# Attention's instruction order: from slots written out per unit to an order made by a list scheduler at build time

## The chip, the cores and the metric

The kernel runs on one core of one Trainium2 chip. The time is the device time of one execution in microseconds. The kernel before took 3646.02 us, the median of 3 runs (3645.23 to 3649.91).

## The reference

One post-norm transformer layer, in float32, on x of shape 2 x 2048 x 1024:

```python
q  = (x @ Wq) as 32 heads of 32;   k, v = x @ Wkv   # one shared key/value head of 32
scores = q k^T / sqrt(32) + slope[head] * (key - query), causal
a  = softmax(scores) @ v                            # then concatenated to 1024
x  = layernorm(x + a @ Wo)
x  = layernorm(x + x @ W^T + b + lora(x))           # lora: one of 4 ranks, chosen per token by a gate
```

## The kernel before

**Work and stages.** The kernel has two parts, one after the other: `attention` and `feed_forward`. Only `attention` changes. It is cut into 64 *units*. A unit `g` is 512 queries (a *segment*, `seg_of(g) = g // 8`) by 4 heads; there are 8 segments (4 for each of the 2 sequences) with 8 units each. Because of causality a unit of the s-th segment of its sequence (s = 0, 1, 2, 3) has `ktiles(g)` = 4, 8, 12 or 16 key tiles of 128 keys. The prediction calls these the four quarters; each quarter occurs twice, so each has 16 units. The last 4 key tiles of a unit lie on the diagonal and have 512, 384, 256 and 128 live query columns.

**What a unit does.** All matrix products are made of a high and a low part to reach float32 accuracy.

1. *Projection* `Q`: q for 4 heads, 8 chunks of the model dimension times 3 products, 24 products of 512 columns, into the bank `ps_m` (L782 to L784, `three`). ScalarE takes the high part (`QE`, L565), VectorE the low part (L671); SyncE copies it within `qst` by DMA.
2. *Maxima* `A`: q times all keys with queries on the partitions, only to find the row maximum (L816, banks `ps_a`), 16 products per segment of keys. VectorE reduces each (L682; on the diagonal with a mask, L685). `CV` and `CT` (L691, L823, L697) turn the result into a shift row, sent by a small DMA.
3. *Scores* `S`: for each key tile and head one product with keys on the partitions (L895, banks `ps_s`, at times `ps_m` as a third), plus a mask product on the diagonal (L898). ScalarE takes the exponential into one of 8 probability tiles `prob` (L603).
4. *Value products* `PV`: per key tile a group of 4 heads, each head on its own 32 columns of the array (128 x 32 weights `val`), float32 in two passes: 8 matmul rows (L828, `ps_o`).
5. *Sums of probabilities*: the same shape with ones for weights (L828, `ps_sum`). `SM` sums one key tile. `SP` sums a pair that GpSimd has added before (`ADD`, L540), `SQ` a quad made of two added pairs (`ADDQ`, L545). A probability tile is free again when its sum is done (`sm_done`, waited for by ScalarE at L602).
6. *End*: ScalarE copies `ps_o` (`OE`, L608), VectorE inverts the sums (`R`), GpSimd multiplies (L521), SyncE stores.

In the sixth unit of a segment x of the next segment is transposed as well (`X`, L777, through the `ps_a` banks), and its keys and values are projected into `ps_m` (`KV`, `VT`). Near the end the 8 pieces of Wo are split into high and low parts (`WO`, L594, L751).

**What sets the order.** Each engine takes its instructions strictly in the order of its queue. `plan_unit(g)` writes that order for one unit; all engines walk the same list and pick what is theirs. The backbone is one score product per slot. Everything else is hung at slots by tables with one entry per quarter: `Q_AT`, `QE_AT`, `A_END`, `A_FROM`, `CHUNKS_AHEAD`, `PV_AT`, `SM_AT`, `WS_AT`, `KV_AT` and others. While unit `g` makes its scores, maxima of `g + 1` (and some of `g + 2`) and the projection of `g + 2` are made. A value product stands after the score of head `PV_AT` of the next key tile, the sum after that of head `SM_AT`:

```python
PV_AT = (1, 1, 2, 1)
SM_AT = (2, 1, 2, 1)
QUADS = (0, 0, 0, 1)   # quads per unit in each quarter; further pairs: pairs_summed
```

With `pairs_summed(g)` = 0, 3, 5, 7 the number of sum groups per unit is 4, 5, 7 and 8. A projection enters the queue as 3 products at a time, the keys' and values' 24 in one piece. `score_places()` fixes which bank each score goes to.

The functions that the diff touches, with the line numbers of the profile:

## Time and profile before

| | |
|---|---|
| median of 3 runs | 3646.02 us |
| profiled execution: span of its instructions | 3641.2 us |
| attention, to the last value product | 2789 us |
| preparation of the feed-forward part | 81 us |
| its 32 tiles of tokens | 771 us |
| TensorE, VectorE, ScalarE, GpSimd busy | 96%, 63%, 51%, 39% |
| granted TensorE clock, mean | 0.988 |

The profile comes from one execution. For it there is the span from the first to the last instruction, 3641.2 us; no separate device time is given, so its own time is this span beside the median of the runs, which is 4.8 us above it. TensorE (PE) rows have modelled ends: two neighbouring products can overlap in the rows, and only the distance from start to start tells what one costs. PEld is the loading of weights, which overlaps with products. A wait is written as *who <- released by whom*. GpSimd is POOL, VectorE DVE, ScalarE ACT; L numbers are lines of the kernel.

### The profile page before, as it was taken

The numbers are of one execution on the slowest core, as the hardware profiler recorded it, in microseconds if no ns is written. First come the engines' busy times: TensorE is split into PE (matmuls) and PEld (weight loads), VectorE is DVE, ScalarE is ACT, GpSimd is POOL, SyncE is SP. The second block draws the span as 40 slices with busy tenths as digits, with TensorE's granted clock in tenths as the row PEclk, the third lists the DMA queues.
The fourth block names the chain that finished last, engine by engine and source line by source line (L and its number), as shares of the span: only waits on it lengthen the run. The fifth ranks groups of instructions, "written<-read, shape, count | busy, mean of one in ns | idle before, by whom it ended". The sixth has DMA issues, their size and how long they took to land. (4 is left out here: it accounts for less than half of the span.)

```text
span 3641.2 us, 56102 instructions
## 1 busy us (share of the span) xinstructions
PE 3481.5 (96%) x20833; PEld 2190.3 (60%) x20833; DVE 2290.6 (63%) x5375; ACT 1866.5 (51%) x3188; POOL 1431.2 (39%) x435
## 2 busy tenths in 40 slices
PE   5999999999999999999999999999998999999998
PEld 4555555555454554555555555454544899999997
DVE  4577777776777772677777776777762444455444
ACT  2546656665667666546656665667675101111100
POOL 1115444554657556115444554657574101011010
PEclk8999999999999999999999999999998999999999
DMA  2221110001000010221110000000012122121221
GB/s 79 55 61 30 35 48 24 25 24 42 18 19 19 19 41 19 57 62 30 36 48 24 24 24 19 19 19 18 13 58 83 47 69 65 56 69 56 65 69 41
DMA packets 158395, 148.33 MB, mean 41 GB/s; under 512 B 9396, under 2 KB 141492, under 8 KB 156056
## 3 DMA queue, kind: packets, MB, share of 16 engines
q1 hardware_dynamic: 158168, 145.34, 13.5%
q8 instruction: 139, 2.28, 0.3%
q14 instruction: 88, 0.72, 0.1%
HBM read 94.39 MB, written 33.62 MB: 35 GB/s over the span
## 5 line engine op out<-in xcount | busy, mean ns | idle before, releaser
L603 ACT ACTIVATE prob<-ps_s,alibi 128x512 f32<-128x512 f32 (+3 forms) x2119 | 1287.2, 633 | 741.6 <-PE ps_s L895 377.9
L540 POOL TENSOR_TENSOR prob<-prob 128x2048 f32<-128x2048 f32 (+1 forms) x240 | 1047.8, 4369 | 977.7 <-ACT prob L603 977.4
L682 DVE TENSOR_REDUCE mxp<-ps_a 128x1 f32<-128x512 f32 x1536 | 978.5, 682 | 296.0 <-PE ps_a L816 284.2
L816 PE MATMUL ps_a<-wol,qst 97*128 97x512 f32 (+3 forms) x2560 | 954.8, 395 | 37.0 <-DVE mxp L685 17.6
L895 PE MATMUL ps_s<-qst,kexp 97*128 97x512 f32 (+3 forms) x2119 | 862.7, 411 | 44.2 <-ACT prob L603 28.5
L895 PEld LDWEIGHTS ps_s<-qst,kexp 97*128 97x128 f32 x2119 | 399.0, 189 | 563.8 <-ACT prob L603 321.5
L685 DVE CUSTOM_DVE_ANT_0 ps_a<-ps_a,maska 128x128 f32<-128x128 f32 (+3 forms) x1024 | 492.4, 507 | 243.8 <-PE ps_a L816 233.3
L828 PE MATMUL ps_o<-prob,val 128*32 128x512 f32 (+3 forms) x5120 | 603.5, 543 | 9.9 <-ACT prob L603 6.6
L816 PEld LDWEIGHTS ps_a<-wol,qst 97*128 97x128 f32 x2560 | 486.5, 194 | 112.7 <-DVE mxp L685 31.9
L1089 POOL TENSOR_TENSOR work<-work,bias_b 128x1024 f32<-128x1024 f32 x32 | 76.9, 2402 | 745.4 <-DVE work L1228 710.9
L828 PE MATMUL ps_sum<-prob,ones 128*32 128x512 f32 (+2 forms) x3072 | 332.5, 505 | 3.7 <-POOL prob L540 3.3
L514 POOL TENSOR_TENSOR wol<-wq_raw,wol 128x1024 fp32r<-128x1024 f32 x64 | 152.5, 2383 | 449.8 <-ACT wol L558 449.8
L603 ACT ACTIVATE prob<-ps_m,alibi 128x512 f32<-128x512 f32 (+3 forms) x441 | 255.2, 579 | 116.6 <-PE ps_m L898 75.0
L1113 ACT ACTIVATE root<-var 128x1 f32<-128x1 f32 x64 | 13.0, 203 | 581.6 <-DVE var L1172 581.6
L1295 PE MATMUL ps_z<-wth,hth 128*128 128x364 f32 x768 | 255.6, 333 | 5.4 <-DVE htl L1250 5.4
L1297 PE MATMUL ps_z<-wtl,hth 128*128 128x364 f32 x768 | 252.8, 329 | 0.0
L1299 PE MATMUL ps_z<-wth,htl 128*128 128x364 f32 x768 | 252.8, 329 | 0.0
L782 PE MATMUL ps_m<-woh,wol 128*128 128x512 f32 x576 | 232.3, 403 | 3.2 <-DVE woh L646 2.8
L784 PE MATMUL ps_m<-woh,wol 128*128 128x512 f32 x576 | 230.0, 399 | 0.0
L783 PE MATMUL ps_m<-woh,wol 128*128 128x512 f32 x576 | 228.9, 397 | 0.0
L671 DVE SCALAR_TENSOR_TENSOR qst<-ps_m,qst 32x512 fp32r<-32x512 f32 x256 | 176.1, 688 | 80.0 <-ACT qst L565 73.4
L828 PEld LDWEIGHTS ps_o<-prob,val 128*32 128x32 f32 x5120 | 105.7, 108 | 188.1 <-ACT prob L603 119.8
(129 smaller groups left out, 3994.7 us busy)
## 6 DMA issues: line engine op xcount, KB each, us to landing
wq_raw<-in_L_attn_Wq SPq DMA_DIRECT2D x64, 512.0 KB, 3.5
work<-in_L_attn_hidden_states SPq DMA_DIRECT2D x8, 2048.0 KB, 8.3
qst<-qst SPq DMA_DIRECT2D x64, 256.0 KB
att_scratch<-at_sb SPq DMA_DIRECT2D x64, 256.0 KB, 2.8
at_raw<-att_scratch SPq DMA_DIRECT2D x32, 512.0 KB, 5.2
work<-in_L_attn_hidden_states SPq DMA_DIRECT2D x32, 512.0 KB, 4.1
out<-work SPq DMA_DIRECT2D x32, 512.0 KB, 3.1
work<-in_L_attn_Wo SPq DMA_DIRECT2D x8, 512.0 KB, 4.1
```

The lines of the kernel that those rows point to most:

```text
L540: nc.gpsimd.tensor_tensor(even[:, :, c1:], even[:, :, c1:], odd[:, :, c1:], ALU.add).then_inc(pair_done, 1)
L603: nc.scalar.activation(prob[slot_of(steps + k)][:, h, c0:], ps_s[places[GH * (steps + k) + h][0]][:, c0:], ACT.Exp, bias=alibi_of(g, h, k ...
L682: nc.vector.tensor_reduce(top, ps, AX.X, ALU.max).then_inc(a_done, 1)
L685: nc.vector.tensor_tensor_reduce(ps, ps, maska[:, QB - cols:], 1.0, MASKED, ALU.add, ALU.max, top).then_inc(a_done, 1)
L782: nc.tensor.matmul(ps, wh, mh, start=start, stop=False)
L784: return nc.tensor.matmul(ps, wl, mh, start=False, stop=stop)
L816: last = nc.tensor.matmul(ps[:, 0:cols], qst[buf][0:KR, h, t * P:(t + 1) * P], kmax[0:KR, ring(sg):ring(sg) + cols], start=True, stop=True)
L828: last = nc.tensor.matmul(ps[h * DH:(h + 1) * DH, c0:], weights, prob[slot_of(steps_before(g) + k)][:, h, c0:], start=k == 0, stop=k == kt ...
L895: last = nc.tensor.matmul(bank[:, c0:], kexp[0:KR, at:at + P], qst[g % 3][0:KR, h, c0:], start=True, stop=not diagonal)
L1295: nc.tensor.matmul(ps, hth[:, c], wth[:, c, piece(p)], start=c == 0, stop=False, skip_group_check=True)
L1297: nc.tensor.matmul(ps, hth[:, c], wtl[:, c, piece(p)], start=False, stop=False, skip_group_check=True)
L1299: last = nc.tensor.matmul(ps, htl[:, c], wth[:, c, piece(p)], start=False, stop=False, skip_group_check=True)
```

## The change

`plan_unit`, `score_places` and their tables go. A class `Order` makes one list of items for all units and all engines at build time. It keeps a clock for each engine, the time at which each bank, probability tile and loaded weight is free, and puts down one piece after the other: for TensorE whatever `choose` names next, for the other engines what follows from it (`push` at the time when its input is ready by the builder's own constants). The instructions that an item issues are those of before, with these differences:

- `QUADS` is (0, 0, 1, 2).
- The 24 products of a projection, of q as of keys and values, are 24 items.
- Value products and sums are taken in batches; a score or a maximum goes to whichever bank of its kind is free first, with the waits for that bank's last user; `ps_m` serves as third score bank when no projection needs it within 2 us.
- The five VectorE steps of the keys (`take_kv`) are five items, with a gap of 700 ns between them; so are the heads of q (300 ns), transposes of x (500 ns) and pieces of Wo (4 us).
- `stack_in` is split into `slopes_in` and `stack_in`; `invert` has two more waits; maxima of a unit may start as soon as its q is there, up to two units ahead of the scores.

```diff
-CHUNKS_AHEAD = (7, 14, 18, 19)
-... (all the tables, chunks_ahead, third_from, score_places, plan_unit)
-QUADS = (0, 0, 0, 1)
+QUADS = (0, 0, 1, 2)
+class Order:
+    S_BANKS, A_BANKS, M_BANK = (0, 1), (2, 3, 4), 5
+    FILL, DRAIN, LOAD, MODE_IN, MODE_OUT = 0.4567, 163, 104, 93, 90
+    SHORT, BATCH, MOST, PACE, MARGIN = 30, 3, 5, 30, 2000
+    LOOK, NARROW_SLACK = 100, 50
+    QE_GAP, X_GAP, K_GAP, WO_GAP = 300, 500, 700, 4000
+    def wide(self, at, length):
+        begin = max((max(self.pe + self.MODE_OUT, at) if self.narrow else max(self.began, at)) + self.LOAD, self.pe)
+        self.narrow, self.began, self.pe = False, begin, begin + length
+        return begin + max(length, 60) + self.DRAIN
+    def columns(self, at, n):
+        begin = max(self.pe + (0 if self.narrow else self.MODE_IN), at + 30)
+        self.narrow, self.began, self.pe = True, begin, begin + 2 * (n * 0.833 + 7)
+        return self.pe + 165
+    def m_open(self):
+        return not self.m_held and self.project_from() > self.pe + self.MARGIN
+    def do_s(self):
+        g, k, h = self.s_unit, self.s_tile // GH, self.s_tile % GH
+        at, bank = self.s_from()
+        n = QB - max(0, k - full_tiles(g)) * P
+        end = self.wide(at, n * self.FILL)
+        ...
+        took = 263 + 0.83 * n
+        done = self.on_act(at, took, took - 106)
+        self.bank_at[bank], self.bank_of[bank] = done, ("e", self.scored)
+    def do_add(self, at, g, i):
+        self.put("ADD", g, i)
+        done = self.on_pool(at, 3465 if 2 * i + 1 > full_tiles(g) else 4588)
+        ...
+    def choose(self):
+        s, a = self.s_from()[0], self.a_from()[0]
+        pv, sums = self.pv_from(), self.sum_from()
+        kv, x = self.kv_from(), self.x_from()
+        q = kv if kv < self.NEVER else self.q_from()
+        job = self.do_kv if kv < self.NEVER else self.do_q
+        ct = max(self.ct_at, self.bank_at[self.pick(self.A_BANKS)] + 54)
+        if self.narrow and pv <= self.pe + self.NARROW_SLACK:
+            return self.take("PV", self.do_pv)
+        if self.narrow and sums <= self.pe + self.NARROW_SLACK:
+            return self.take("PV", self.do_sum)
+        edge = self.SHORT + (self.pe + self.MODE_OUT if self.narrow else self.pe - self.LOAD)
+        if ct <= edge: ...
+        if self.v_from <= edge: ...
+        if x <= edge and self.pe - self.x_began > self.X_GAP: ...
+        left = 3 * DC - (self.kv_next if kv < self.NEVER else self.q_next)
+        urgent = q <= edge and self.ahead() * 466 < left * 700 + self.PACE * 466
+        n = self.waiting() if pv <= self.pe + 90 else 0
+        if n >= self.MOST or n >= self.BATCH and s > edge and a > edge:
+            return self.take("PV", self.do_pv if pv <= sums else self.do_sum)
+        if urgent and self.before != "Q":
+            return self.take("Q", job)
+        if s <= edge and (a > edge or self.before != "S"):
+            return self.take("S", self.do_s)
+        if a <= edge:
+            return self.take("A", self.do_a)
+        if q <= edge:
+            return self.take("Q", job)
+        first = min((max(s + self.LOAD, self.pe), 0), (max(a + self.LOAD, self.pe), 1),
+                    (max(q + self.LOAD, self.pe), 2), (max(min(pv, sums) + 30, self.pe + self.MODE_IN), 3),
+                    (max(x + self.LOAD, self.pe), 4), (ct + self.LOAD, 5), (self.v_from + self.LOAD, 6))
+        ...
-            for what, arg in plan:          # on each engine, unit by unit
+            for what, n, arg, bank, before, at in items:     # on each engine, once over all units
+                if what == "S":
+                    bank_free(before)
+                    scores(n, *arg, banks[bank])
+                ...
+            def project(wh, wl, m):
+                j, part = m // 3, m % 3
+                return nc.tensor.matmul(ps_m[:], (wl if part == 2 else wh)[:, j], (xl if part == 1 else xh)[:, j],
+                                        start=m == 0, stop=m == 3 * DC - 1)
```

## Rows read from the trace of the kernel before

**Rows 1.** The page's busy table: busy us, share of the span, instructions.
```profile
PE 3481.5 (96%) x20833; PEld 2190.3 (60%) x20833; DVE 2290.6 (63%) x5375; ACT 1866.5 (51%) x3188; POOL 1431.2 (39%) x435
```
**Rows 2.** Windows: stretch, its length, busy us of each engine, granted clock, DMA.
```profile
0.00:2789.00 2789.00, 2658.65 (x16433) 1440.68 (x16433) 1875.73 (x4368) 1772.04 (x3017) 1352.75 (x398) 0.99 0.12 34
0.00:74.00 74.00, 35.27 (x143) 27.78 (x143) 32.79 (x147) 13.39 (x20) 10.01 (x18) 0.85 0.30 97
263.00:550.00 287.00, 275.29 (x1756) 156.95 (x1755) 206.49 (x495) 183.10 (x313) 129.97 (x40) 0.99 0.14 39
1442.00:1628.00 186.00, 173.83 (x1180) 105.38 (x1180) 124.05 (x365) 100.09 (x185) 28.94 (x16) 1.00 0.21 58
2316.00:2789.00 473.00, 459.15 (x2774) 225.91 (x2765) 301.93 (x612) 331.39 (x558) 307.81 (x77) 1.00 0.10 29
2789.00:2870.00 81.00, 65.28 (x324) 56.68 (x317) 34.67 (x59) 17.07 (x21) 6.30 (x7) 0.83 0.30 91
2870.00:3641.20 771.20, 757.58 (x4086) 692.96 (x4084) 380.18 (x948) 77.36 (x151) 72.13 (x30) 0.99 0.19 60
```
**Rows 3.** Groups by line and shape on TensorE: count, busy us, mean ns, idle before.
```profile
L816 PE MATMUL ps_a<-wol,qst 97*128 97x512 f32 x1792 | 743.2, 431 | 17.6 <-DVE mxp L685 10.1 <-DVE mxp L682 4.6 <-DMA qst<-qst 1.2
L895 PE MATMUL ps_s<-qst,kexp 97*128 97x512 f32 x1555 | 676.2, 439 | 42.7 <-ACT prob L603 28.0 <-DMA qst<-shift_t 9.3
L828 PE MATMUL ps_o<-prob,val 128*32 128x512 f32 x3584 | 482.0, 610 | 2.8 <-ACT prob L603 1.0
L828 PE MATMUL ps_sum<-prob,ones 128*32 128x512 f32 x1920 | 253.4, 600 | 3.7 <-POOL prob L540 3.3 <-POOL prob L545 0.2
L782 PE MATMUL ps_m<-woh,wol 128*128 128x512 f32 x576 | 232.3, 403 | 3.2 <-DVE woh L646 2.8 <-DVE val L665 0.4
...
L895 PE MATMUL ps_m<-qst,kexp 97*128 97x512 f32 x237 | 103.2, 435 | 2.0 <-ACT prob L603 1.7
```
**Rows 4.** TensorE's timeline in a fourth-quarter unit: start us, us, instruction.
```profile
2442.33 0.40 PE L782 MATMUL ps_m<-woh,wol 128*128 128x512 f32 x1
2442.56 0.40 PE L783 MATMUL ps_m<-woh,wol 128*128 128x512 f32 x1
2442.80 0.40 PE L784 MATMUL ps_m<-woh,wol 128*128 128x512 f32 x1
2443.12 1.07 PE L828 MATMUL ps_o<-prob,val 128*32 128x512 f32 x8
2444.12 0.50 PE L895 MATMUL ps_s<-qst,kexp 97*128 97x512 f32 x1
2444.46 0.39 PE L816 MATMUL ps_a<-wol,qst 97*128 97x512 f32 x1
```
**Rows 5.** The same view where two narrow groups follow each other.
```profile
1010.35 1.07 PE L828 MATMUL ps_sum<-prob,ones 128*32 128x512 f32 x8
1011.23 0.40 PE L828 MATMUL ps_o<-prob,val 128*32 128x128 f32 x8
```
**Rows 6.** Waits: who waited for whom, us in total, times, longest.
```profile
ACT prob L603 <- PE ps_s L895: 377.9, 534, 8.6
...
PEld ps_s L895 <- ACT prob L603: 321.5, 509, 1.0
...
PEld ps_o L828 <- ACT prob L603: 119.8, 385, 1.3
```
**Rows 7.** Groups by line and shape on GpSimd and VectorE.
```profile
L540 POOL TENSOR_TENSOR prob<-prob 128x2048 f32<-128x2048 f32 x192 | 880.6, 4590 | 925.7 <-ACT prob L603 925.7
L682 DVE TENSOR_REDUCE mxp<-ps_a 128x1 f32<-128x512 f32 x1536 | 978.5, 682 | 296.0 <-PE ps_a L816 284.2
```
**Rows 8.** A window of one fourth-quarter unit, columns as in rows 2.
```profile
2437.00:2497.00 60.00, 59.73 (x361) 30.70 (x357) 43.03 (x89) 41.87 (x70) 39.10 (x10) 1.00 0.07 19
```
**Rows 9.** The first score products of two successive first-quarter units, TensorE's timeline.
```profile
159.34 0.50 PE L895 MATMUL ps_s<-qst,kexp 97*128 97x512 f32 x1
...
180.17 0.51 PE L895 MATMUL ps_s<-qst,kexp 97*128 97x512 f32 x1
```

More of the change, by code:

```diff
@@ L82, in quads_summed @@
     return QUADS[seg_of(g) % NSEG]
-def adds_in(g):
-    return pairs_summed(g) + quads_summed(g)
-def adds_before(g):
-    return sum(adds_in(x) for x in range(g))
-def adds_until(g, k):
-    pair = k // 2
-    quad = pair // 2
-    if quad < quads_summed(g):
-        return adds_before(g) + 3 * quad + 1 + pair % 2
-    return adds_before(g) + quads_summed(g) + pair + 1
 def ring(sg):
@@ L329, in attention @@
         ps_m = pb(ctx, "ps_m", [P, QB])
-        ps_s.append(ps_m)
-        places = score_places()
+        banks = ps_s + ps_a + [ps_m]
+        items = Order([max(n for n in range(FIRST) if n % 3 == i) for i in range(3)]).made()
         counters = []
@@ new lines, in add_quad @@
+            def add_quad(g, i, adds):
+                one, two = (prob[slot_of(steps_before(g) + 4 * i + o)] for o in (0, 2))
+                pool.wait_ge(pair_done, START + adds)
+                nc.gpsimd.tensor_tensor(one[:], one[:], two[:], ALU.add).then_inc(pair_done, 1)
+            for number in range(3):
+                split_wq(number)
+            for what, n, arg, bank, before, at in items:
+                if what == "WL":
+                    split_wq(n)
+                if what == "DIV":
+                    divide(n)
+                if what == "ADD":
+                    add_pair(n, arg)
+                if what == "ADDQ":
+                    add_quad(n, arg, at)
@@ new lines, in scores @@
+            def scores(g, k, h, bank):
+                if (k, h) == (0, 0):
+                    pe.wait_ge(c_in, START + 16 * (g + 1))
+                c0 = max(0, k - full_tiles(g)) * P
+                diagonal = k >= full_tiles(g)
+                at = key_tile(g, k) * P
+                last = nc.tensor.matmul(bank[:, c0:], kexp[0:KR, at:at + P], qst[g % 3][0:KR, h, c0:],
+                                        start=True, stop=not diagonal)
+                if diagonal:
+                    last = nc.tensor.matmul(bank[:, c0:c0 + P], identb[:], maskt[:], start=False, stop=True)
+                last.then_inc(s_full, 1)
@@ L917, in _, with values, sums @@
-            units(prologue, step, lambda count: None)
+            def values(g, k):
+                pe.wait_ge(e_done, START + GH * (steps_before(g) + k + 1))
+                if k == 0:
+                    pe.wait_ge(o_copied, START + g)
+                    pe.wait_ge(vt_done, START + seg_of(g) + 1)
+                over_keys(g, ps_o, val[:, key_tile(g, k)], k).then_inc(pv_done, 1)
+            def sums(g, k, tiles, adds):
+                if k == 0:
+                    pe.wait_ge(sum_turned, START + g)
+                if tiles == 1:
+                    pe.wait_ge(e_done, START + GH * (steps_before(g) + k + 1))
+                else:
+                    pe.wait_ge(pair_done, START + adds)
+                over_keys(g, ps_sum, ones[:], k).then_inc(sm_done, tiles)
```

1012 lines of the change are left out of this document (625 added, 387 removed).

## The prediction

> **What bounds the kernel now.** I read the busy table of the page first [rows 1]: TensorE is busy 96% of the span. Then the stages [rows 2]. Attention ends at 2789 us; the feed-forward part behind it (81 us of preparation and 771 us of steady work) is not touched. In each attention stage TensorE is 93 to 98% busy, and ScalarE is under 71% and VectorE under 72% of the same stretches. So TensorE's queue sets the time of attention, and the question is what it is busy with. The ends of its rows are modelled, so I count starts instead [rows 3, 4, 5].
>
> A 512-column product in the ordinary shape follows its neighbour by 0.233 us (2442.33 to 2442.56 to 2442.80). A row of 8 narrow ones (4 heads side by side, two passes; I call the 8 a group) takes 0.88 us when another group follows at once (1010.35 to 1011.23). A group by itself costs more: the product of 2442.80 should give way at 2443.03, the group starts at 2443.12, the next score product at 2444.12, and that one is followed only 0.34 us later, at 2444.46, where 0.233 is usual. From 2443.03 to 2444.46 less one 0.233 is 1.20 us. So every run of groups, however long, costs 0.32 us besides the groups; I take 0.31, since the group's start was also held by an exponential.
>
> The account of attention. Ordinary products: 3584 full ones for maxima and scores (1792 each) and 1728 of the projections [rows 3]; the narrower ones of the diagonal (512 each of 384, 256 and 128 columns, from the code) make 768 more in full widths: 6080 x 0.2335 = 1420 us. The 1024 masks and the 256 transposes, 128 columns each, by proportion 75 us. Narrow groups: 5504 rows of full width are 688 groups, the diagonal's are worth 156: 844 x 0.88 = 743 us. Together 2238 us. Runs: PV_AT and SM_AT put a value product at every step of 4 scores and the sums beside it, in the first quarter even apart from it: 7, 8, 12 and 16 runs a unit in the four quarters, 43 x 16 = 688 runs, x 0.31 = 213 us. From 2789 that leaves 338 us; 39 of them lie in the first 74 us, where TensorE is busy 35 [rows 2]. The other 299 us are waits that the busy rows cover.
>
> The list of waits says on whom: weight loads of scores wait for the exponential that frees their bank, value products for the exponential of the step just before [rows 6]; and in turn ScalarE waits for scores. No engine is short: the fixed slots ask for things a moment too early.
>
> At this point the busy share and the starts give different limits. Busy rows cover 2659 of the 2789 us of attention [rows 2], so by them at most 130 us of idle could be had, and the 28 us of work below: 3646 - 158 = 3488. The Trainium skill ("Perfetto Trace Analysis", Identifying the Most-Contended Engine) says that TensorE's matmul occupancy is a poor measure of the distance to the roofline and that weight-load occupancy is better; by weight loads [rows 1] TensorE stands at 60%. The rows bear this out: in rows 4 the busy row of 0.50 us stands for 0.34 us of start distance. The sum here goes by the starts in any case.
>
> **The change, part by part.** The profiled span is 3641.2 us, the median of the runs 3646.02, so 4.8 us lie around it; I take the differences off the median.
>
> (a) QUADS goes from (0, 0, 0, 1) to (0, 0, 1, 2). A quad sum takes the place of two pair sums on TensorE: one full group less per unit in the third and fourth quarters, 32 x 0.88 = 28 us. It costs GpSimd 32 more additions of 4.59 us [rows 7], 147 us in all, spread over 32 units. In a fourth-quarter unit GpSimd goes from 39.1 of 60 us [rows 8] to 43.7. That is beside TensorE's work as long as probability tiles come free in time (below).
>
> (b) Runs. The new builder starts value products when 3 tiles wait and neither a score nor a maximum can start, at once at 5, and stays with narrow work while any is ready; but its last rule also starts it with fewer, when the next ordinary product would come later than the narrow one. 640 value groups at 3 to 5 a run would make 130 to 210 runs; one at a time 640. I take 1.5, 3, 5 and 7 a unit, 16.5 x 16 = 264: shorter batches than 3 in the late quarters, because there ScalarE needs 41.9 of 60 us [rows 8] and TensorE will often find no free bank. 424 runs less x 0.31 = 131 us. Bounds: 400 runs (89 us) and 183 (157 us).
>
> (c) Waits. From the account a fourth-quarter unit has 140 full widths x 0.2335 + 0.9 + 21.25 groups x 0.88 = 52.3, and 16 runs 5.0, against the 60 us of the unit in rows 8: 2.7 us of waits. A first-quarter unit is 20.8 us from first score to first score [rows 9]; 44 widths x 0.2335, 0.9, 5 groups x 0.88 and 7 runs make 17.8: 3.0 us. For the two quarters between I take 2.9. 11.5 x 16 = 184 us; the other 115 us of the 299 then lie at the changes of segment (transposing x, keys and values) and at the ends. The builder asks for a product only when its bank is free by its own constants, and these are near the rows: 682 ns for a full maximum and 4588 for a pair addition, where rows 7 have 682 and 4590. Single projection products (0.233 us each, 24 a unit) fill holes that a block of three or six made or missed. Bounds: nothing gained, where an in-order queue misses as often as now, and nearly all of it, 250 us. I take half in the steady units (1.5 us left in each, 88 us gained) and 55 us of the 115, since the chain x, keys, q, DMA is still a chain and has new gaps written into it (300 to 700 ns between parts). Together 143 us.
>
> Nothing is added on the other engines but the 32 additions. Wait instructions are different but not more per product. The splitting of stack_in into two counters lets slopes go ahead of the copies of q; both are SyncE issues of which none is near TensorE. Wo's split moves to its own pace, 8 pieces of about 6.3 us (1.06 on ScalarE, 1.22 on VectorE and a gap of 4.0, by its constants), 50 us inside two units of 50 us; were it late, each piece would push the feed-forward part by some 6 us. A third score bank is now taken only when no projection needs it within 2 us; what is late next in the late quarters is ScalarE.
>
> Sum: 28 + 131 + 143 = 302 us; 3646 - 302 = 3344 us.
>
> **The rivals.**
> (A) ScalarE and VectorE starve during batches. A batch of 3 value groups and one or two sums is about 4 us; two or three score banks cover 1.2 to 1.8 us of it. A fourth-quarter unit then needs ScalarE's 41.9 and, of 17.8 us narrow work, what is not covered: with 5 runs 17.8 - 7.5, 52 us, just under TensorE's 53.6 (52.3 less 0.9, and 7 runs); with the cover of one bank only (0.7 us by the builder's constant) 56 us. For: ScalarE's 70% and GpSimd's 65% there [rows 8]. Against: the chooser goes for a score first. Price: (c) gives nothing in the third and fourth quarters and half elsewhere, and the runs stay near 400: 28 + 89 + 50 = 167, 3480 us; this is also where the limit by busy rows would put it. I give 3410 to 3560.
> (B) Nearly all waits go: 28 + 150 + 240 = 418, 3228 us. For: no engine but TensorE is above 72%. Against: DMA landings vary, and one late product holds the whole queue.
> (C) Slower: the ring of 8 probability tiles. A quad holds 4 tiles until its three additions (3 x 4.6 = 13.8 us) and the sum behind them are done, and the first addition waits for the value product of its tile. If that comes at once after 3 steps of 3.75 us, the sum can run at about 11.3 + 0.9 + 13.8 = 26 us, and the ring turns in 8 x 3.75 = 30: free. If the batch waits for 5 tiles and the sum for the next batch, it is 18.8 + 0.9 + 13.8 + 11 = 44.5, and exponentials stop for 14 us. There are 48 quads; the case is slower from 302 / 48 = 6.3 us a quad, and at 8 us the time is 3344 + 384 = 3728. Against it: a stopped score leaves TensorE with nothing ordinary, and then the narrow work goes at once.
> (D) It doesn't do what it says: runs hardly fewer, since the last rule starts narrow work whenever TensorE would idle about 0.1 us. Then 28 us and a little of (c): 3600.
>
> **Chances.** Forecast 3344 (3275 to 3410) 0.52; A 0.24; B 0.15; C 0.04; D 0.05 (0.02 of it within 0.2%). Range 3235 to 3465: it holds the forecast, most of B and the near half of A. 0.2% is 7 us, about what a measurement of this kernel can tell. Faster by more than that 0.94, within it 0.02, slower 0.04.
>
> **What would show it.** (a) 352 instead of 384 sum groups (2816 narrow rows on ps_sum, not 3072), 288 additions on GpSimd. (b) Narrow rows in runs: 200 to 330 runs; if over 450, D. (c) A fourth-quarter unit at 55 us, a first-quarter one near 17.7; waits of score weight loads for exponentials down from 400 us to under 200. A: long idle of ScalarE behind narrow runs, waits for ps_s as large as now. C: ScalarE waiting for a sum product (sm_done). The feed-forward stretch must stay at 771 us; if it moves by more than 3 us, something that I left out matters.

## The result and the profile after

The changed kernel takes 3601.39 us (median of 4 runs, 3597.28 to 3604.0), the kernel before 3645.62 us beside it: ratio 0.9874, 95% interval 0.9861 to 0.9886. It is 44 us faster where I forecast 302, and outside my range (3235 to 3465). All of it lies in attention, which ends at 2747 us instead of 2789; the two later stages kept their 81 and 771 us, as forecast.

The busy table and windows after (the columns are those of [rows 1, 2]):

```profile
PE 3428.3 (95%) x20577; PEld 2225.1 (62%) x20577; DVE 2313.2 (64%) x5375; ACT 1822.1 (51%) x3188; POOL 1576.9 (44%) x467
```

```profile
0.00:2747.00 2747.00, 2605.47 (x16177) 1475.53 (x16177) 1898.31 (x4368) 1728.29 (x3017) 1498.53 (x430) 0.97 0.12 34
280.00:560.00 280.00, 273.55 (x1748) 159.58 (x1749) 202.95 (x484) 174.13 (x310) 126.89 (x39) 0.97 0.13 38
1414.00:1614.00 200.00, 181.16 (x1219) 113.03 (x1219) 117.95 (x334) 101.82 (x191) 32.90 (x18) 0.93 0.19 55
2283.00:2747.00 464.00, 448.40 (x2740) 232.43 (x2738) 319.60 (x625) 327.23 (x560) 344.77 (x85) 0.99 0.09 28
2747.00:2828.00 81.00, 65.31 (x324) 56.65 (x317) 34.68 (x59) 16.50 (x20) 6.28 (x7) 0.83 0.31 90
2828.00:3599.10 771.10, 757.50 (x4086) 692.88 (x4084) 380.26 (x948) 77.34 (x151) 72.07 (x30) 0.99 0.19 60
```

Against [rows 2] the second first-quarter stretch became slower (186 to 200 us), and its clock fell from 1.00 to 0.93. A steady fourth-quarter unit gained, the last three units of the first segment lost; both windows of the kernel after, and the second one's counterpart before:

```profile
1108.00:1166.20 58.20, 57.62 (x355) 30.89 (x353) 43.00 (x90) 40.95 (x70) 43.52 (x11) 1.00 0.07 19
175.20:280.30 105.10, 85.49 (x524) 54.01 (x523) 60.42 (x154) 44.12 (x80) 14.57 (x8) 0.88 0.18 55
```

```profile
180.20:262.70 82.50, 77.15 (x499) 47.54 (x495) 59.94 (x160) 40.15 (x75) 10.84 (x6) 0.98 0.22 65
```

The steady unit takes 58.2 us (60 in [rows 8]; 55 forecast). The steady first-quarter units take 20.0 us in the mean (21.0 before, 17.7 forecast). Over all segments, the first five units of each gained 91 us; the last three, in which the segment changes, lost 50.

The groups on TensorE: 1664 + 512 + 512 + 128 = 2816 rows on `ps_sum`, 352 groups, as step (a) said (the diagonal's are the last three):

```profile
L1201 PE MATMUL ps_sum<-prob,ones 128*32 128x512 f32 x1664 | 222.9, 609 | 1.1 <-POOL prob L887 1.1
...
L1201 PE MATMUL ps_sum<-prob,ones 128*32 128x256 f32 x512 | 39.5, 379 | 0.0
...
L1201 PE MATMUL ps_sum<-prob,ones 128*32 128x128 f32 x512 | 25.9, 273 | 0.0
...
L1201 PE MATMUL ps_sum<-prob,ones 128*32 128x384 f32 x128 | 13.4, 489 | 0.0
```

Counted from the starts of all rows, narrow work now comes in 463 runs; it was 688, and my forecast was 264. (The recorded expectations count one run fewer in every order of the builder.) And this is what became of the waits of [rows 6] (who waited for whom, us, times, longest):

```profile
PEld ps_s L1192 <- ACT prob L931: 151.1, 345, 1.6
...
PEld ps_a L1178 <- DVE mxp L1038: 74.2, 182, 4.1
...
PEld ps_a L1178 <- DVE mxp L1041: 53.2, 134, 3.8
PEld ps_m L1192 <- ACT prob L931: 50.9, 76, 1.5
```

Before, the maxima's two rows were

```profile
PEld ps_a L816 <- DVE mxp L685: 31.9, 61, 1.2
...
PEld ps_a L816 <- DVE mxp L682: 25.2, 64, 1.4
```

The scores' waits for exponentials fell from 400 us (321.5 and 78.6, the second one for `ps_m`) to 202, about what the prediction had named as the sign of success ("under 200"), but those for the maxima's banks rose from 57 to 127 us. A sign that I had chosen came true, and the time didn't follow.

The account by the prediction's own pitches, an estimate. Attention got 42 us shorter. Groups give 28 and 225 fewer runs 70; so everything else grew by 56 us. Half clock is more than all of that: from 80 us to the last value product the granted clock stands at 0.5 (1.2 GHz) for 154 us, 20 before; at twice the pitch that costs (154 - 20) / 2 = 67 us. Of step (c), forecast at 143 us, some 11 are left.

By place the two parts of each segment differ. The forecast is split 40 to 24 by units, and the 55 us of the changes of segment go to the last three:

| us | first five units of each segment | last three |
|---|---|---|
| forecast: groups, runs, waits | 18 + 82 + 55 = 155 | 11 + 49 + 33 + 55 = 148 |
| measured | 91 gained | 50 lost |
| groups, by 0.88 | 18 | 11 |
| fewer runs, by 0.31 | 42 (430 to 293 runs) | 27 (258 to 170) |
| half clock | -9 (18 to 36 us of it) | -57 (7 to 122) |
| what is left for waits | 40 | -31 |

(Half clock is counted from the first score at 73 us here, which adds 5 us to both kernels; rounding and 1 us ahead of that score make the difference to the 11.) In the steady units the waits gave 40 us of the 55 that I had put there. In the last three they and the clock took 88 us, where I had forecast 88 gained.

### The profile page after: what moved, and what is told of

The parts are those of the page before. It is cut to its first block and busy times, and to the rows that moved or that the text cites. A ratio compares the mean times of both kernels' runs of the same rounds, so it can differ in the third digit from the quotient of the medians.

```text
span 3599.1 us, 55753 instructions
## 1 busy us (share of the span) xinstructions
PE 3428.3 (95%) x20577; PEld 2225.1 (62%) x20577; DVE 2313.2 (64%) x5375; ACT 1822.1 (51%) x3188; POOL 1576.9 (44%) x467
## 3 DMA queue, kind: packets, MB, share of 16 engines
q1 hardware_dynamic: 158168, 145.34, 13.6%
## 5 line engine op out<-in xcount | busy, mean ns | idle before, releaser
L931 ACT ACTIVATE prob<-ps_s,alibi 128x512 f32<-128x512 f32 (+3 forms) x2091 | 1236.7, 628 | 633.7 <-PE ps_s L1195 300.4
L1178 PE MATMUL ps_a<-wol,qst 97*128 97x512 f32 (+3 forms) x2560 | 971.9, 400 | 47.1 <-DVE mxp L1038 17.9
L1192 PE MATMUL ps_s<-qst,kexp 97*128 97x512 f32 (+3 forms) x2091 | 815.9, 394 | 25.7 <-DMA qst<-shift_t 14.6
L1145 PE MATMUL ps_m<-woh,wol 128*128 128x512 f32 x1728 | 670.7, 423 | 9.7 <-DVE qst L1027 5.1
L1201 PE MATMUL ps_o<-prob,val 128*32 128x512 f32 (+3 forms) x5120 | 574.7, 546 | 13.8 <-ACT prob L931 7.2
L1145 PEld LDWEIGHTS ps_m<-woh,wol 128*128 128x128 f32 x1728 | 335.9, 199 | 69.0 <-issue 11.8
L931 ACT ACTIVATE prob<-ps_m,alibi 128x512 f32<-128x512 f32 (+3 forms) x469 | 285.1, 608 | 184.5 <-PE ps_m L1195 108.3
L1201 PEld LDWEIGHTS ps_o<-prob,val 128*32 128x32 f32 x5120 | 133.5, 109 | 255.6 <-issue 153.8
L1201 PE MATMUL ps_sum<-prob,ones 128*32 128x512 f32 (+3 forms) x2816 | 284.4, 501 | 1.1 <-POOL prob L887 1.1
L887 POOL TENSOR_TENSOR prob<-prob 128x2048 f32<-128x2048 f32 x48 | 221.0, 4604 | 3.8
```

What stands on the lines that cost most here:

```text
L887: nc.gpsimd.tensor_tensor(one[:], one[:], two[:], ALU.add).then_inc(pair_done, 1)
L931: nc.scalar.activation(prob[slot_of(step)][:, h, c0:], bank[:, c0:], ACT.Exp, bias=alibi_of(g, h, k - full_tiles(g))).then_inc(e_done, 1)
L1145: return nc.tensor.matmul(ps_m[:], (wl if part == 2 else wh)[:, j], (xl if part == 1 else xh)[:, j], start=m == 0, stop=m == 3 * DC - 1)
L1178: last = nc.tensor.matmul(bank[:, 0:cols], qst[g % 3][0:KR, h, t * P:(t + 1) * P], kmax[0:KR, ring(sg):ring(sg) + cols], start=True, stop= ...
L1192: last = nc.tensor.matmul(bank[:, c0:], kexp[0:KR, at:at + P], qst[g % 3][0:KR, h, c0:], start=True, stop=not diagonal)
L1201: last = nc.tensor.matmul(ps[h * DH:(h + 1) * DH, c0:], weights, prob[slot_of(steps_before(g) + k)][:, h, c0:], start=k == 0, stop=k == kt ...
```

## The experiments

All medians are compared by their ratio to the kernel before, timed on the same chip (3644 to 3650 us). "Planned end" is where the order builder's own clock ends TensorE's list: 2493.5 us for the change. In the text the gains are differences of medians; "half clock" is the time at 0.5 from 80 us to the last value product (the first 80 us have 15 to 34 in every run). The kernel before differs by up to 5.5 us from chip to chip, so a difference of a few us between kernels that were not timed side by side (e1 to e4; e5 to e8; e9 to e12; e13 to e16; e17 and e18) is not told apart.

| | median us | ratio, 95% interval | runs | half clock |
|---|---|---|---|---|
| e1 keys' copy on ScalarE | 3570.26 | 0.9790 [0.9776, 0.9803] | 461 | 119 |
| e2 quads as before | 3613.46 | 0.9905 [0.9890, 0.9920] | 437 | 150 |
| e3 no batches | 3739.86 | 1.0255 [1.0241, 1.0269] | 662 | 201 |
| e4 kernel before, new quads | 3699.11 | 1.0149 [1.0133, 1.0164] | 688 | 89 |
| e5 = e1, x loaded later | 3567.62 | 0.9785 [0.9768, 0.9803] | 461 | 116 |
| e6 = e1, keys' products in one piece | 3556.76 | 0.9754 [0.9737, 0.9770] | 482 | 102 |
| e7 = e1, q in threes | 3623.82 | 0.9939 [0.9922, 0.9955] | 512 | 157 |
| e8 = e5 and e6 | 3566.24 | 0.9782 [0.9766, 0.9799] | 482 | 99 |
| e9 = e6, Wo on GpSimd | 3549.07 | 0.9737 [0.9724, 0.9751] | 485 | 89 |
| e10 = e9, measured constants | 3545.73 | 0.9721 [0.9708, 0.9734] | 487 | 78 |
| e11 = e6, extra products | 3576.41 | 0.9803 [0.9789, 0.9816] | 482 | 92 |
| e12 = e6, half exponentials | 3559.78 | 0.9763 [0.9749, 0.9778] | 482 | 94 |
| e13 = e10, 896 masks less | 3495.82 | 0.9586 [0.9570, 0.9602] | 487 | 75 |
| e14 = before, 896 masks less | 3606.27 | 0.9879 [0.9859, 0.9899] | 688 | 58 |
| e15 = e10, half maxima | 3524.64 | 0.9662 [0.9646, 0.9678] | 487 | 79 |
| e16 = e10, both halves | 3512.18 | 0.9630 [0.9613, 0.9648] | 487 | 88 |
| e17 = e10, fewer runs | 3559.34 | 0.9749 [0.9731, 0.9766] | 365 | 116 |
| e18 = e10, far fewer runs | 3700.51 | 1.0139 [1.0122, 1.0156] | 268 | 322 |

### The change taken apart: e1 to e4

**e1.** The trace after had a plain stop: behind the keys' projection, VectorE copies the keys (0.42 us by itself), and four of the eight copies took 3.3 to 4.7 us. VectorE's rows by shape (count, total, mean), and the second such place on the timeline:

```profile
L1017 DVE CAST wol<-kexp 96x512 fp32r<-96x512 f32 x8 | 17.7, 2208 | 0.2
```

```profile
1275.11 4.52 POOL L882 TENSOR_TENSOR prob<-prob 128x2048 f32<-128x2048 f32 x1 [5.32 <-ACT prob L931]
1275.17 4.73 DVE L1017 CAST wol<-kexp 96x512 fp32r<-96x512 f32 x1
...
1279.83 1.27 DVE L1038 TENSOR_REDUCE mxp<-ps_a 128x1 f32<-128x512 f32 x2
...
1280.05 0.60 PE L1160 MATMUL ps_m<-ident,vt_sb 32*128 32x32 f32 x4 [3.73 <-DVE wol L1017]
```

```profile
1280.00:1286.80 6.80, 6.75 (x30) 4.08 (x30) 4.76 (x8) 3.44 (x5) 0.00 (x0) 0.58 0.00 0
```

GpSimd's addition ends at 1279.63, the copy 0.27 us later; in all four cases the copy started while an addition ran and ended 0.27 to 0.29 us behind it. TensorE stands for 3.73 us, and the window behind it shows a granted clock of 0.58. Before, the same eight copies took 0.422 to 0.424 us, none beside an addition. The reductions of maxima around it, which read `ps_a`, keep their 0.68 us beside additions ([rows 7], and 683 ns in the mean after). The Trainium skill ("SBUF — State Buffer", Who interferes with whom) says that copies and casts on VectorE can contend with GpSimd for a pair of ports that one instruction holds alone until it ends, and that a reduction never does: the trace agrees with both. The edit gives the copy to ScalarE:

```diff
-nc.vector.tensor_copy(kmax[0:3 * DH, cols], kexp[0:3 * DH, cols].bitcast(F32)).then_inc(kv_done, 1)
+nc.scalar.activation(kmax[0:3 * DH, cols], kexp[0:3 * DH, cols].bitcast(F32), ACT.Copy).then_inc(kv_done, 1)
```

> The changed kernel, but the last of the five steps of the keys (the copy of kexp into kmax, from SBUF to SBUF) is made by ScalarE and not by VectorE. Theory 1: in the changed kernel this copy, 0.42 us by itself, stands for 3.3 to 4.7 us at four of the seven changes of segment, each time until a GpSimd addition that began before it ends; the holes of TensorE in front of the transposes of v (2.2, 3.7, 3.2 and 2.7 us, 11.8 in all) come from it, and behind each the granted clock falls to half for some 7 us, which loses up to 3.4 us more. Expected: holes gone, the time 10 to 25 us below the changed kernel, near 3583. Rival: what is late at the change of segment is the chain of single products and gaps itself; then the next link waits instead and the time stays within 5 us of 3601.

31 us faster than the change, more than the 10 to 25 expected; the copies on ScalarE take 0.62 us each. The stops were 11.7 us, and the time at half clock fell from 154 to 119 us, some 17 us of loss: together 29 of the 31. That the copy stands for the addition is shown, and that taking it away is worth 31 us in all. How much of the clock's part belongs to these four stops is not: e1 has another list behind the first change of segment, and half clock went at other places too.

**e2, e4.** `QUADS` back to (0, 0, 0, 1) in the change, and (0, 0, 1, 2) in the kernel before.

> The changed kernel with QUADS back at (0, 0, 0, 1): 32 narrow groups more on TensorE, 32 additions less on GpSimd. If the quads are worth their products, the time rises by 28 us or a little less, to about 3625. Rival: the quads hold 4 of the 8 probability tiles too long or crowd GpSimd (now 72% busy in the fourth quarter), so that they cost what they save: then it stays within 8 us of 3601 or falls below it.

> The kernel before with nothing changed but QUADS = (0, 0, 1, 2). 32 groups of 0.88 us less on TensorE: 28 us faster, about 3618, if GpSimd and the ring of tiles follow. Rival: at fixed slots the sum of a quad (slot of step 7, 11) waits for GpSimd's third addition and holds the queue: gain under 10 us or a loss.

In the change the quads are worth 12 us, not 28. Some of the difference is the order: e2's list has 26 runs fewer, 8 us by 0.31, and its planned end is 14 us later. In the kernel before the quads cost 53: the sum of a quad stands at a fixed slot, before GpSimd has it. TensorE's waits there (for the addition that makes the quad, L545) are 69 us, and were 0.2, and half clock rose from 20 to 89 us:

```profile
PEld ps_sum L828 <- POOL prob L545: 40.8, 14, 4.2
PE ps_sum L828 <- POOL prob L545: 28.6, 14, 3.3
```

So the new table is only good with the new order. My step (a) had priced the additions as free beside TensorE, which only holds where the order gives them time.

**e3.** `BATCH, MOST = 1, 1` in place of 3, 5.

> The changed kernel with BATCH and MOST at 1: a value product goes as soon as one tile waits. By its own list 661 runs of narrow groups in place of 462. Theory: a run costs TensorE 0.31 us whatever stands in it, so 199 more runs cost 62 us: about 3663, and slower than the kernel before if nothing else of the change gains. Rival A of the prediction (batches starve ScalarE and VectorE): the time rises by less than 30 us, because their waits get shorter.

138 us slower with 199 more runs, over twice the 62 of a pitch of 0.31. The batches are what the change lives on, but the price is not the runs' pitch alone: the planned end is 122 us later (2493.5 to 2615.4), so the builder's clock has nearly all of it. It knows no half clock, of which there is 47 us more.

### Changes of segment: e5 to e9, e11

The transposed keys `VT` come 27.7 us behind the first product of the keys' projection at the first change of segment (199.2 to 226.9 us), where it was 9.6 (202.0 to 211.6). Over the seven changes it is 18.6 to 39.5 us, 26 in the mean, and was 9.6 to 20.1, 14 in the mean: the 24 products are no longer one piece and a gap of 700 ns stands between VectorE's steps. At 205.42 the trace also shows TensorE waiting 4.62 us for the shift row's DMA, which SyncE issued 1.3 us behind the load of x:

```profile
205.42 0.76 PE L1192 MATMUL ps_s<-qst,kexp 97*128 97x512 f32 x1 [4.62 <-DMA qst<-shift_t]
```

```profile
196.96 0.37 SPq L783 DMA_DIRECT2D work<-in_L_attn_hidden_states  x1
198.28 0.53 SPq L803 DMA_DIRECT2D qst<-shift_t  x1
```

```diff
-self.push(end, self.do_x_load, sg + 1, self.a_made)              # e5: x 20 us later
+self.push(end + 20000, self.do_x_load, sg + 1, self.a_made)
-QE_GAP, X_GAP, K_GAP, WO_GAP = 300, 500, 700, 4000               # e6
+QE_GAP, X_GAP, K_GAP, WO_GAP = 300, 0, 0, 4000
+dense = kv < self.NEVER and q <= edge                            # e6: the keys' 24 at once
-if urgent and self.before != "Q":
+if dense or urgent and self.before != "Q":
-job = self.do_kv if kv < self.NEVER else self.do_q               # e7: q three at a time
+job = self.do_kv if kv < self.NEVER else self.do_three
```

> The kernel of e1 with the 2 MB load of the next segment's x put into SyncE's list 20 us later (it isn't needed for 100 us or more). In the changed kernel the shift row of unit 6 was issued 1.3 us behind that load and landed so late that TensorE stood 4.6 us in front of the unit's first score, and the clock halved for 10 us. Theory: small DMAs behind the big one are late: 5 to 12 us faster than e1's 3570. Rival: the shift row is late for its own reasons: within 3 us.

> The kernel of e1 with the 24 products of keys and values in one piece as soon as they can go, and without the gaps of 700 and 500 ns between the steps of the keys and the transposes of x. Theory 2: at a change of segment TensorE waits for the chain x, keys, v, q, maxima; single products between others and the gaps make it longer (keys' first product to v's transposes 27.7 us in the changed kernel at the first change, 9.6 before). Expected: that distance back to 9 to 12 us, 15 to 30 us faster than e1. Rival: the chain isn't what TensorE waits for, or what is gained in it is lost by the products that it displaces: within 5 us of e1.

> The kernel of e1 with q's products put down three at a time, as before the change, all else by the builder. If single products are what fills the small holes between scores and maxima, three in a row delay a score each time: by the builder's own list 511 runs in place of 460, 16 us at 0.31 us, and waits on top: 25 to 45 us slower than e1. Rival: three in a row cost nothing (the score banks cover 0.7 us): within 10 us.

> e5 and e6 together on e1: if both theories hold the gains add, 20 to 40 us below e1, near 3540, and the time at half clock in attention falls from 140 us to under 100. If neither, 3570.

e5: the stop is gone and the time the same within its interval: a stop of 4.6 us at one place is no gain of 4.6 us. e6: 13.5 us, just short of the 15 expected. The distance at the first change is 14.1 us and not 9 to 12, over all seven 11.5 to 16.9, as before the change; the chain counts, though it is a small part of what was missing. e7: 54 us slower than e1, which is 76 faster than the kernel before; single projection products between scores and maxima are most of what this order gains (42 of the 54 us stand in the planned end as well). e8 is 9.5 us slower than e6 and not faster. Its list for TensorE is e6's, item for item, as e5's is e1's; only SyncE issues the load of x later. TensorE's waits for shift rows at the scores rose from 7.1 us in 2 waits to 11.9 in 4: the late load may have got into the way of others, but half of the 9.5 us is not accounted for.

**e9** gives the low parts of Wo to GpSimd, since in the change VectorE's eight pieces also stood beside additions (3.11 us each, 1.71 before), with two stops of TensorE of 4 us. **e11** puts six unread products ahead of the first maximum of a unit in the first quarter and at changes of segment.

```diff
-nc.vector.tensor_tensor(wol[:, c], xs[:, c % QT], woh[:, c].bitcast(F32), ALU.subtract)      # e9
+nc.gpsimd.tensor_tensor(wol[:, c], xs[:, c % QT], woh[:, c].bitcast(F32), ALU.subtract)
+for _ in range(6):                                                                          # e11
+    nc.tensor.matmul(bank[:], kexp[0:KR, at:at + P], kexp[0:KR, at:at + QB], start=True, stop=True)
```

> The kernel of e6 (keys' copy on ScalarE, the 24 products of keys and values in one piece) with the eight low parts of Wo made by GpSimd instead of VectorE. Theory: what is left of the loss by copies on VectorE that stand until a GpSimd addition ends are these eight (24.9 us for 8 in the changed kernel, 1.2 each when undisturbed) and two TensorE stops of 4 us at about 2607 and 2628 us; on GpSimd they can't overlap an addition, so 8 to 15 us go: 3542 to 3549 against 3557. Rival: Wo's split is beside the path and the two stops only move, or GpSimd's own queue delays pair sums: within 3 us of 3557.

> e6 with six extra products of 512 columns, whose results nobody reads, into the free bank of maxima ahead of the first maximum of a unit in the first-quarter stretches and at every change of segment. Theory: the waits there are followed by stretches at half clock (126 us of attention in e6, about 55 us of loss), and work that fills the waits keeps the clock: half clock falls under 80 us and the time by 5 to 15 us, to 3542 to 3552. Rival: the clock isn't what costs there, the extra work only stands in the queue, up to 1.4 us for each of some 24 units: 5 to 30 us slower, 3562 to 3587.

e9: 7.7 us, at the edge of the 8 to 15 expected, and half clock fell from 102 to 89. e11: 20 us slower. Half clock fell from 102 to 92 and not under 80, and the extra products cost more than that gives. Filling waits with work is no remedy here.

### What TensorE waits for: e10, e12 to e16

e10 sets the builder's constants to measured values (beside the six that its text names, a narrow pass is planned 4.7 ns shorter). e12 and e15 halve what ScalarE and VectorE do for each bank, e16 both; e13 and e14 take mask products out of e10 and of the kernel before.

```diff
-FILL, DRAIN, LOAD, MODE_IN, MODE_OUT = 0.4567, 163, 104, 93, 90                # e10, one of six
+FILL, DRAIN, LOAD, MODE_IN, MODE_OUT = 0.4567, 163, 104, 93, 113
+c1 = c0 + (QB - c0) // 2                                                       # e12, e16
-nc.scalar.activation(prob[slot_of(step)][:, h, c0:], bank[:, c0:], ACT.Exp,
+nc.scalar.activation(prob[slot_of(step)][:, h, c0:c1], bank[:, c0:c1], ACT.Exp,
+half = max(P, cols // 2)                                                       # e15, e16
-ps, top = bank[:, 0:cols], mxp[:, h * QT + t, c:c + 1]
+ps, top = bank[:, cols - half:cols], mxp[:, h * QT + t, c:c + 1]
-diagonal = k >= full_tiles(g)                                                  # e13, e14
+diagonal = k >= full_tiles(g) and g % HG == 0
```

> e9 with six of the builder's constants set to what the traces show: first narrow pass of a run 24 ns longer, leaving a run 113 ns instead of 90, a diagonal maximum that finds VectorE idle 150 ns later, the shift row 2300 instead of 1870, the copy of q 2900 instead of 2600, the gap between heads 150 instead of 300. Theory: the builder's clock runs ahead of the chip (2493 us planned, about 2670 real), so every item of which it believes that its bank is free comes a little early and TensorE's queue holds; right constants would give back 10 to 30 us against e9. Rival: order is good enough and the drift comes from stretches at half clock and single late DMAs that no constant holds: within 4 us of e9.

> e6 in which ScalarE takes each exponential over the first half of the live columns only (the rest of a probability tile stays at 1.0 from one setting at the start; this changes what is computed). The order is the same. Theory that ScalarE's return of score banks is what TensorE waits for in the steady units: an exponential is some 200 ns shorter, and more than 60 us go. Rival: ScalarE has slack (70% busy), and what TensorE waits for are its own order, the chain at a change of segment and VectorE: under 15 us.

> e10 in which VectorE reduces each block of maxima over half its columns only, at least 128 (what is computed changes): 682 ns become about 400. Theory that TensorE waits for VectorE's return of the banks of maxima: over 30 us go. Rival: VectorE has slack as ScalarE has, and the order asks for a bank no sooner: under 10 us.

> e10 with both halves, the exponentials' and the maxima's (what is computed changes). Theory: each engine hides behind the other, and only with both quick do the waits go: over 60 us. Rival: what is left isn't waiting for banks at all but fixed pitches of short products, the chains at changes of segment and half clock: under 20 us.

e10 gained 3.3 us, the rival's answer: the order is not waiting for better constants of this kind. e12: nothing (3 us slower than e6), though a full exponential went from 688 to 474 ns. The waits show why: those of scores for exponentials fell and those for maxima rose. e12 (first fence) and e6 (second):

```profile
PEld ps_s L1206 <- ACT prob L938: 104.8, 145, 1.2
...
PEld ps_a L1192 <- DVE mxp L1052: 91.7, 238, 4.1
...
PEld ps_a L1192 <- DVE mxp L1055: 67.4, 161, 4.5
```

```profile
PEld ps_s L1199 <- ACT prob L932: 150.8, 343, 1.6
...
PEld ps_a L1185 <- DVE mxp L1045: 72.2, 169, 4.1
...
PEld ps_a L1185 <- DVE mxp L1048: 58.8, 149, 2.1
```

e15 gained 21 us and e16 33.5, between what theory and rival had: VectorE's return of banks is worth some 20 us, both engines' together 34. That is a tenth of the 299 us that I had called waits in the kernel before; more than that faster partners did not give, in this order.

**What else the 299 us were.** The timeline of the kernel before in the fourth quarter:

```profile
2246.85 0.39 PE L895 MATMUL ps_m<-qst,kexp 97*128 97x512 f32 x1
2247.08 0.23 PE L898 MATMUL ps_m<-maskt,identb 128*128 128x128 bf16 x1
2247.12 0.48 PE L816 MATMUL ps_a<-wol,qst 97*128 97x512 f32 x1
2247.44 0.39 PE L895 MATMUL ps_s<-qst,kexp 97*128 97x512 f32 x1
2247.67 0.23 PE L898 MATMUL ps_s<-maskt,identb 128*128 128x128 bf16 x1
```

The mask product of 2247.08 is followed after 0.04 us, so I priced it at that. But the maximum behind it is followed after 0.32 us instead of 0.233. Over the whole trace that lateness is not spread as waits are: behind a mask and a full maximum it is 81 to 84 ns in most cases, whatever comes next. All that comes late behind mask products (their neighbour's successor) adds up to 70 us in the kernel before and 82 in the one after, and behind the transposes of x to 15 and 12.

> e10 without the mask product behind a diagonal score in 7 of 8 units (896 of 1024 go; what is computed changes). Everything else is in the same order. By the distance of 41 ns from a mask product to the next start, which is what my account gave it, 37 us go. Theory: the product after a mask product's neighbour starts 81 to 84 ns late in the trace (mask, maximum, then a score 0.318 us behind the maximum where 0.233 is usual), in the same few nanoseconds every time, so it is a fixed pitch of the short product and not a wait: 896 x 0.125 = 112 us by that, 85 to 125 us go. Rival: the 84 ns are waits for banks that come back elsewhere: 30 to 50 us.

> The kernel before without the same 896 mask products. Theory: the cost was the same fixed one there, so that some 85 us of the 299 that the prediction put down to waits were none: 70 to 125 us go. Rival: 37 us.

e13 gave 50 us and e14 38: both times of the rival, at the upper edge of its range and at its number, and neither of the theory. The traces show both parts of it. In e14 the lateness behind masks went from 70 to 8 us, as the theory has it. But the same starts, behind ordinary products, are 38 us later in all than before (142 to 179 us), and half clock went from 20 to 58 us, some 19 of loss: 37 + 62 - 38 - 19 = 42 us, against 38 measured. In e13 the lateness behind masks fell by 69 us against e10 and that behind ordinary products rose by 43. The lateness is a fixed pitch, since it goes with the masks; most of what it frees comes back as waits and half clock, so as time it is worth no more than the rival said. That is the same give and take as in e12.

### Runs: e17, e18

```diff
-(max(min(pv, sums) + 30, self.pe + self.MODE_IN), 3)
+(max(min(pv, sums) + 30, self.pe + self.MODE_IN) + 100 * (self.waiting() < self.BATCH), 3)   # e18: 300
```

> e10 with 100 ns laid on narrow work in the last rule of the choice while fewer than 3 value groups wait, so that an ordinary product that comes up to 100 ns later is preferred. The list then has 364 runs instead of 486. By the prediction's step (b), 122 runs fewer at 0.31 us are 38 us: 3508. By the builder's own clock, whose end goes from 2514 to 2523, what the runs give TensorE pays back as waits: 9 us slower, 3555. Between them, 3525 to 3540, part of the price of a run is saved.

> The same with 300 ns: 267 runs, the number that the prediction had forecast for the change (264). By its step (b) 219 runs fewer than e10 are 68 us: 3478. By the builder's own clock (2514 to 2651) TensorE has too often nothing else that is ready, and the kernel gets 137 us slower: 3683. If it is over 3600, so few runs were not to be had together with full score and maxima banks, and the forecast of 264 had no order behind it.

With my 264 runs (e18 has 268) the kernel is 155 us slower than e10 (the builder's clock said 137), not 68 faster. With 365 it is 13.6 us slower (10 by the ratios; builder: 9). The waits of e18, and TensorE's timeline at the longest:

```profile
ACT prob L941 <- PE ps_s L1204: 386.6, 163, 33.2
...
PEld ps_a L1187 <- DVE mxp L1054: 167.6, 498, 1.2
```

```profile
874.23 27.49 PE L1187 MATMUL ps_a<-wol,qst 97*128 97x512 f32 x47
901.65 1.94 PE L1210 MATMUL ps_o<-prob,val 128*32 128x512 f32 x8
903.36 4.53 PE L1210 MATMUL ps_sum<-prob,ones 128*32 128x512 f32 x24
907.82 0.49 PE L1201 MATMUL ps_s<-qst,kexp 97*128 97x512 f32 x1
```

Where narrow work is held back, TensorE waits for VectorE's maxima (168 us in 498 waits, 68.5 in 183 in e10), and the clock is at half for 322 us, 78 in e10. At five places the rule goes further: with fewer than 3 value groups waiting it prefers one maximum after the other, 28 to 47 in a row at VectorE's pace (27.5 us for 47 in the rows above), while no score is made; only the narrow groups behind them let the scores go on. ScalarE stands for 21 to 33 us each time, 143 us in all, against 9.3 us at most in e10. The 200 maxima and 20 groups made in these 143 us would take 64 at 0.233 and 0.88 us. So by an estimate 79 us, half of e18's loss, are this stop and not the price of few runs as such. e18 shows that so few runs are not to be had by this rule; for the order in general e17 is the better witness.

## Why the prediction was wrong, step by step

**The bound** was right: TensorE's queue sets attention's time, the feed-forward stretch didn't move, and no other engine became the bound. **The account** of [rows 3 to 5] was wrong in what it left over. Of 299 us "waits", some 85 us are the fixed lateness behind mask products and transposes (70 and 15), and some 10 half clock. That is the trace's count; as time, taking 896 masks away gave 38 us in the kernel before (e14), of which my account had 37.

**(a), 28 us.** The count was right (352 groups; 240 additions of pairs and 48 of quads, 288), the price was not: 12 us by e2. That the additions are free depends on the order: in the old one they cost 53 us net (e4).

**(b), 131 us.** 463 runs instead of 264. I took the number from the sizes 3 and 5 and gave the last rule, which I had read, too little weight; it starts narrow work whenever the next ordinary product would come later, and 400 runs were my worst bound. By 225 runs at 0.31 us the step gave 70 us, an estimate, since no run has the old runs in the new order with all else the same. e17 shows that it was no oversight of the builder: 122 runs fewer cost 13.6 us and don't save 38. e18 says the same more loudly, but half of its loss is the stop described there. A run is a cost and also what fills a wait; I had priced only the first.

**(c), 143 us.** About 11 came, and this is the step that failed most, nearly all of it in the last three units of each segment. In the first five I forecast 55 us from waits, and 155 with (a) and (b); all three brought 91. By the account above the waits gave 40, and the clock took 9. The waits for exponentials were halved as I said, and those for maxima more than doubled. In the last three I forecast 148 us gained in all and 50 were lost. I had taken the new order's waits there as half of the old ones' and named its gaps without a price. The runs showed a longer chain of keys and values (e6: 13.5 us), copies on VectorE that stand behind GpSimd's additions (e1 31 us, e9 8 us), and half clock. From the change to e10 these last three units get 62 us shorter and the first five 5 us longer, so what the repairs brought lies all there.

**Not priced at all:** the granted clock, some 67 us, 57 of them in the last three units of each segment. Before, 26 starts of TensorE come over 0.9 us late (29 us in all) behind 80 us, the longest 3.2 us late in the last unit; after, 31 with 64 us, up to 5.0. After, 17 of 23 stretches at half clock begin beside a stop, 6 do not; before, 5 of 6 do not.

**The rivals.** D said that with over 450 runs the time would be 3600, by 28 us and a little of (c). The time and the number of runs came out like that, and D's mechanism, the last rule, fits the run count; but "hardly fewer" is not true (225 runs went), and e3 shows that without batches it would have been 3740. That D's 3600 is so close is luck: the 42 us are 28 + 70 + 11 - 67, and D knew neither the 70 nor the 67. A (3480): the runs stayed near 400 as it said, but ScalarE's starving is not the reason (e12), and with both partners at half work only 34 us went (e16). B is excluded. C did not occur in the change; e18's five stops, where scores rest until waiting groups are made, are the nearest to it.

Best version: e10, 3545.73 us, 0.9721 [0.9708, 0.9734] of the kernel before, 1.5% under the change (3601.39). Its parts are the change, the keys' copy on ScalarE (31), the keys' products in one piece (13.5), Wo's low parts on GpSimd (8) and constants (3, at the edge of what the runs tell apart).

**Open:** what makes up the steady units' remaining distance. In e16 with both partners quick it takes 33 us less, so most of the rest is in the order or in pitches that I haven't measured one by one. Why the later load of x costs 9.5 us in e8 and nothing in e5 was not settled, nor which activity takes the clock down in stretches that begin without a stop: one at 2261.9 lasts 17.1 us with TensorE busy for 16.9.

```profile
2261.90:2279.00 17.10, 16.92 (x65) 7.93 (x65) 8.52 (x31) 6.03 (x10) 13.55 (x5) 0.50 0.06 17
```

## What to carry to other kernels

What an account leaves over is not yet a wait: look first whether the lateness has one size (81 to 84 ns behind most mask products) or many; and even a fixed pitch is worth only what the next wait leaves of it (e13, e14). When several engines return banks at nearly the same pace, one row of the list of waits can halve and the time stay, since the next resource takes the wait over; only an experiment that speeds up both says what waits are worth. If work is planned by a builder with its own clock, ask that clock first what a count such as "264 runs" would cost: its planned ends gave 122 for 138 us (e3), 14 for 12 (e2), 42 for 54 (e7), 9 for 13.6 (e17) and 137 for 155 (e18). What it can't see (a shared port, the clock) has to come from the trace: for e1 it gave 4 us of 31, and e9 it called 7 us slower where it was 8 faster. And split a forecast by place: a sum that misses by 260 us here hides steady units that came near and changes of segment that turned from gain to loss.

## What the runs showed of the hardware that I had not expected

- A copy on VectorE with source and target in SBUF, begun while GpSimd adds, ends 0.27 to 0.29 us after the addition (4 of 4): 3.3 to 4.7 us for a copy of 0.42. Eight copies done by ScalarE took 0.62 us each, beside additions or not.
- A mask product (128 columns, bf16) costs its own 41 ns and makes the product after the next some 83 ns late, in all about 0.12 us of pitch. Behind an ordinary product of 128 columns the same start is about 49 ns late (0.282 us for 0.233). Without 896 masks the kernels got 38 and 50 us faster, 0.04 to 0.06 each.
- Entering and leaving the narrow shape costs about 0.31 us a run beyond the groups, but a run is worth having where it fills a wait.
- Beside most stops of TensorE of 0.9 to 5 us the clock stands at half for 3.4 to 13.7 us, but not beside all: in the kernel before, seven stops of 1.0 to 1.3 us have none. The 133 us of it that the change added are worth some 67 us by the pitch at either level.
